# Merged weight products laid after a branch, fetch lists made sooner, first norm on VectorE

## The reference

```
x = x + gelu(layernorm(x) @ ctx.T) @ ctx                     # part 1, per batch
x = x + moe(layernorm(x))                                    # part 2: 8 experts, 256 -> 512 -> 256, one expert per token
x = x + attention(q=layernorm(x), k=v=ctx, 16 heads, mask, distance bias)   # part 3
y = layernorm(x); e = argmax(router(y[:, -1, :]))            # part 4: one expert per batch
x = x + y + 0.3 * ((gelu(y @ W1[e] + b1[e]) @ W2[e] + b2[e]) @ Wo + bo)
```

## Time and profile before

| | |
|---|---|
| median of 3 runs | 701.96 us |
| the profiled execution | 699.54 us, span 697.6 us |
| PE busy | 634.7 us (91%) |
| DVE busy | 325.5 us (47%) |
| ACT busy | 268.8 us (39%) |
| POOL busy | 120.8 us (17%) |
| expert loop, first product to the last pass's end | 284.7 to 370.5 us |
| first query product of attention | 398.88 us |

### The profile page before, as it was taken

The page is one execution under the profiler, slowest core; times in us unless marked ns, Lnnn a source line. Parts: engine busy times, 40 slices in busy tenths (PEclk is TensorE's granted clock), DMA queues, the critical chain, the costliest instruction groups (busy, mean ns, idle before and its releaser), DMA issues.

```text
span 697.6 us, 9158 instructions
## 1 busy us (share of the span) xinstructions
PE 634.7 (91%) x3091; PEld 389.6 (56%) x3093; DVE 325.5 (47%) x1035; ACT 268.8 (39%) x370; POOL 120.8 (17%) x176
## 2 busy tenths in 40 slices
PE   3999999999998779899989668999999989999998
PEld 1666666666666446788878423433433433435665
DVE  4334233103005777122222729768797796752401
ACT  1111111111112233333332256767576577585321
POOL 0000000000002001344452007041022022033310
PEclk9999999999999899999999979999999999999999
DMA  8993301804002314153324395332751600031241
GB/s 306 358 366 117 131 0 68 266 0 155 30 1 75 129 54 145 30 134 122 119 72 144 139 123 84 51 63 44 116 82 25 106 2 3 2 94 43 69 128 60
DMA packets 50086, 70.77 MB, mean 101 GB/s; under 512 B 7472, under 2 KB 39130, under 8 KB 49642
## 3 DMA queue, kind: packets, MB, share of 16 engines
q1 hardware_dynamic: 47898, 64.45, 34.1%
q0 software_dynamic: 2144, 5.77, 3.0%
HBM read 48.48 MB, written 15.13 MB: 91 GB/s over the span
## 4 chain that ended last, share of the span: by engine, by line
PE 70%; DVE 16%; issue 6%; DMA 3%; ACT 2%; POOL 2%; DVEq 0%; POOLq 0%; ACTq 0%; SPq 0%
PE ps L909 14%; PE ps L920 13%; DVE arena L2158 7%; PE ps L1475 6%; PE ps L1089 4%; PE ps L1457 4%; PE ps L1001 4%; PE ps L1200 4%; PE ps L1361 3%; PE ps L1212 3%; PE ps L1097 3%; DVE arena L1874 3%; PE ps L1384 2%; PE ps L1125 1%; PE ps L987 1%
## 5 line engine op out<-in xcount | busy, mean ns | idle before, releaser
L2158 DVE TENSOR_REDUCE arena<-ps 128x1 f32<-128x400 f32 x256 | 129.2, 564 | 41.8 <-PE ps L1361 40.9
L1699 ACT ACTIVATE arena<-ps 100x1024 f32<-100x1024 f32 x128 | 124.0, 1020 | 59.3 <-PE ps L1457 59.1
L909 PE MATMUL ps<-xnT,arena 128*128 128x512 f32 x208 | 102.0, 615 | 0.9 <-DVE xnT L1759 0.9
L920 PE MATMUL ps<-arena 128*128 128x256 f32 x416 | 99.0, 382 | 0.0
L920 PEld LDWEIGHTS ps<-arena 128*128 128x128 f32 x416 | 80.1, 193 | 33.4 <-issue 25.0
L1511 ACT ACTIVATE arena<-ps 128x512 f32<-128x512 f32 x52 | 31.0, 597 | 175.1 <-PE ps L909 175.1
L1361 PE MATMUL ps<-arena 97*128 97x400 bf16 x256 | 76.0, 339 | 6.1 <-DVE arena L2158 2.3
L1457 PE MATMUL ps<-arena 100*100 100x512 bf16 x256 | 75.9, 380 | 0.1
L1475 PE MATMUL ps<-arena 100*32 100x512 f32 x512 | 68.6, 604 | 0.6 <-ACT arena L1699 0.6
L1361 PEld LDWEIGHTS ps<-arena 97*128 97x128 bf16 x256 | 20.4, 97 | 78.2 <-DVE arena L2158 50.1
L909 PEld LDWEIGHTS ps<-xnT,arena 128*128 128x128 f32 x208 | 39.8, 195 | 30.7 <-issue 28.5
(11 more groups left out here) (239 smaller groups left out, 715.9 us busy)
## 6 DMA issues: line engine op xcount, KB each, us to landing
arena<-in_W SPq DMA_DIRECT2D x16, 512.0 KB, 9.2
arena<-in_ctxT SPq DMA_DIRECT2D x4, 1664.0 KB, 8.5
arena<-in_ctxN SPq DMA_DIRECT2D x4, 1664.0 KB, 12.8
arena<-arena SPq DMA_DIRECT2D x48, 128.0 KB
last_k_parts<-arena SPq DMA_DIRECT2D x24, 100.0 KB, 1.8
arena<-last_k_parts SPq DMA_DIRECT2D x8, 300.0 KB
x_tok<-in_x SPq DMA_DIRECT2D x4, 512.0 KB, 9.3
xn_rows<-xn SPq DMA_DIRECT2D x4, 512.0 KB
```

The lines of the kernel that those rows point to most:

```text
L909: ins = pe.matmul(ps[:, 4 + k % 2, :], ctxT_s[:, b % 2, c, f * P:f * P + P], xnT[:, c, S * b:S * b + S], start=(c == 0), stop=(c == KC - 1))
L920: ins = pe.matmul(ps[:, b % 2 * 2 + t // 2, t % 2 * D:t % 2 * D + D], hid[:, (k - 2) % 4, t * P:t * P + P], ctxN_s[:, b % 2, f, :], start= ...
L1699: act.activation(pexp2[0:KT, c % 4, :, :], ps[0:KT, 2 + 2 * (c % 2):4 + 2 * (c % 2), :], ACT.Exp).then_inc(f_pe, 1)
L2158: dve.tensor_reduce(nm2[:, m // MU % 2, h, j:j + 1], ps[:, FAST.bank(x), 0:KF], AX.X, ALU.max, negate=True).then_inc(s_by["dve"], 1)
```

## The change

- Ahead of the loop three merged weights are made instead of four. The fourth, n = 3, follows the loop. n = 4 to 6 stand at the start of the chosen way, behind the branch, in place of the 14 products of `keep_busy`. n = 7 is made after the query products of batch 0 and their splitting. ACT's takes and SP's stores move alike; the store of n = 0 goes ahead of the stores of the keys.
- In the loop DVE makes the list of tokens to fetch after the first W1 copy and not after the second. For that the second copy waits until the first turned block is there.
- POOL runs one pass less in its loop; the last pass has its two scatters alone. SP waits for two fewer loads.
- The norm of batch 0 is applied by DVE and not by ACT, and the two halves of the turned tokens go to banks 6 and 7.
- The bounds given for the value of `pairs` become 8 to 12 from 1 to 12.

```diff
-MERGED_EARLY, MERGED_BIAS = 4, 3
+MERGED_EARLY, MERGED_BIAS, MERGED_LAST = 3, 3, 7
-    early = [(("queries", b, k), 6) for b in range(2) for k in range(KC)]
+    early = [(("queries", b, k), 6 + k) for b in range(2) for k in range(KC)]
...
+            store_merged(0)
             for b in range(B):
                 store_keys(b)
...
-            for n in range(MERGED_EARLY):
-                sp.wait_ge(s_xsb, 32 * (5 + n))
+            for n in range(1, MERGED_EARLY):
+                sp.wait_ge(s_xsb, 32 * (4 + n))
                 store_merged(n)
...
+                store_late_merged()
                 for half in range(2):
                     queries(0, half)
+                store_last_merged()
...
-            sp.wait_ge(s_xsb, pairs * 32 + 64)
+            sp.wait_ge(s_xsb, pairs * 32 + 32)
...
+            def store_late_merged():
+                sp.wait_ge(s_w2s, 16 * (MERGED_EARLY + 1))
+                for n in range(MERGED_EARLY, MERGED_LAST):
+                    store_merged(n)
+
+            def store_last_merged():
+                sp.wait_ge(s_w2s, 16 * (MERGED_LAST + 1))
+                store_merged(MERGED_LAST)
...
             merge_weights(2, 2)
-            pe.wait_ge(s_w2c, merged(1))
-            merge_weights(3, 4)
...
-            merge_weights(4, 2)
+            merge_weights(3, 2)
             pe.wait_ge(s_xsT, pairs * 2 + 2)
             pe.wait_ge(s_expd, 1)
-            merge_weights(5, 4)
-            pe.wait_ge(s_w2c, merged(4))
-            merge_weights(6, 2)
-            pe.wait_ge(s_w2c, merged(5))
-            merge_weights(7, 4)
+
+            def merge_late():
+                merge_weights(4, 4)
+                pe.wait_ge(s_w2c, merged(3))
+                merge_weights(5, 2)
+                pe.wait_ge(s_w2c, merged(4))
+                merge_weights(6, 4)
+
+            def merge_last():
+                pe.wait_ge(s_w2c, merged(6))
+                merge_weights(MERGED_LAST, 4)
...
-                pe.wait_ge(s_gat[0], 16)
-                keep_busy(2)
-                pe.wait_ge(s_moe, 1)
-                keep_busy(8)
-                pe.wait_ge(s_lnst, 2 * 0 + 1)
-                keep_busy(4)
+                merge_late()
                 pe.wait_ge(s_tpf, tp[0])
                 for k in range(KC):
                     make(("queries", 0, k))
                 queries(0)
                 query_rest(0)
                 query_rest(1)
+                merge_last()
                 for k in range(KC):
                     make(("queries", 1, k))
...
-                act.wait_ge(s_w2s, 16 * (E + 1) if b else 16 * (MERGED_EARLY + 1))
+                act.wait_ge(s_w2s, 16 * (MERGED_EARLY + 1, MERGED_LAST + 1, MERGED_LAST + 1, E + 1)[b])
...
             def fast_way():
-                norm(0, 0, 1)
+                take_late_merged()
                 for k in range(KC):
                     take_columns(("queries", 0, k))
                 query_parts()
+                take_merged(MERGED_LAST, 4)
                 norm(1, 0, B)
...
+            def normalize(b):
                 for t in range(TB * b, TB * b + TB):
                     ins = dve.tensor_scalar(xn[:, t, :], x_tok[:, t, :], mv[:, t, 0:1], rstd[:, t:t + 1], ALU.subtract, ALU.mult)
                 ins.then_inc(s_ln, 1)
...
             with dve.Fori(0, pairs) as i:
-                for j in range(2):
-                    dve.wait_ge(s_eh, i * 2 + j + 1)
-                    block_weights(bass.ds(i * 2 + (2 + j), 1), j)
+                dve.wait_ge(s_eh, i * 2 + 1)
+                block_weights(bass.ds(i * 2 + 2, 1), 0)
                 dve.wait_ge(s_xsTr, i * 2 + 3)
                 dve.tensor_scalar(idx_x[:, :], idx[:, bass.ds(i * 2 + 4, 2)], 0.0, None, ALU.add).then_inc(s_idxl, 1)
+                dve.wait_ge(s_eh, i * 2 + 2)
+                block_weights(bass.ds(i * 2 + 3, 1), 1)
...
                 norm_roots(0)
+                if first_norm:
+                    dve.wait_ge(s_w2s, 16 * (MERGED_EARLY + 1))
+                    normalize(0)
                 norm_shifts(0)
...
-            with pool.Fori(0, pairs) as i:
+            with pool.Fori(0, before_last) as i:
...
+            pool.wait_ge(s_idx, before_last + 1)
+            pool.sem_inc(s_turn, 1)
+            for j in range(2):
+                pool.wait_ge(s_eyc, before_last * 2 + j + 1)
+                pool.sem_inc(s_turn, 1)
+                store_answers(j)
```

More of the change, by code:

```diff
@@ L29 @@
 NBLK = 24
-PAIRS = NBLK // 2
+PAIRS, LEAST_PAIRS = NBLK // 2, T // P // 2
 IDX = NBLK + 4
@@ L681, in _ @@
             sp.wait_ge(s_slot, 1)
-            pairs = sp.value_load(be_i[0:1, NBLK:NBLK + 1], min_val=1, max_val=PAIRS)
+            pairs = sp.value_load(be_i[0:1, NBLK:NBLK + 1], min_val=LEAST_PAIRS, max_val=PAIRS)
             sp.wait_ge(s_list, 1)
@@ L828, in _ @@
                 sp.dma_start(yg[:, TB * b:TB * b + TB, :], yt_d[S * b:S * b + S, :].rearrange("(t p) d -> p t d", p=P)).then_inc(s_gat[b], 16)
-            sp.wait_ge(s_w2s, 16 * (MERGED_EARLY + 1))
-            for n in range(MERGED_EARLY, E):
-                store_merged(n)
+            def store_late_merged():
[5 more added lines that the diff above has]
+                store_merged(MERGED_LAST)
             with sp.If(near > 0):
@@ L1075, in _ @@
             pe.wait_ge(s_slot, 1)
-            pairs = pe.value_load(be_i[0:1, NBLK:NBLK + 1], min_val=1, max_val=PAIRS)
+            pairs = pe.value_load(be_i[0:1, NBLK:NBLK + 1], min_val=LEAST_PAIRS, max_val=PAIRS)
             pe.wait_ge(s_w12, 16 * 2 * E)
@@ L1117, in query_products @@
                 if b == 0:
-                    pe.wait_ge(s_w2c, merged(E - 1))
+                    pe.wait_ge(s_w2c, merged(5))
+                if b == 1:
+                    pe.wait_ge(s_w2c, merged(MERGED_LAST))
                 for m in range(KC):
@@ L1553, in _ @@
             act.activation(bo2[:, :], ps[0:E, 0, 0:D], ACT.Copy, scale=0.3).then_inc(s_w2c, 1)
-            for n, bank in ((2, 2), (3, 4)):
-                take_merged(n, bank)
+            take_merged(2, 2)
             act.wait_ge(s_slot, 1)
@@ L1558, in _ @@
                 act.wait_ge(s_ekst[i], 48 * KC * B // 2)
-            pairs = act.value_load(be_i[0:1, NBLK:NBLK + 1], min_val=1, max_val=PAIRS)
+            pairs = act.value_load(be_i[0:1, NBLK:NBLK + 1], min_val=LEAST_PAIRS, max_val=PAIRS)
             with act.Fori(0, pairs) as i:
@@ L1569, in _, with take_late_merged @@
             act.sem_inc(s_expd, 1)
-            for n, bank in ((4, 2), (5, 4), (6, 2), (7, 4)):
-                take_merged(n, bank)
+            def take_late_merged():
+                for n, bank in ((3, 2), (4, 4), (5, 2), (6, 4)):
+                    take_merged(n, bank)
             act.wait_ge(s_list, 1)
@@ L1754, in layer_norm @@
                 ins.then_inc(s_ln, 1)
+            def layer_norm(b):
+                norm_roots(b)
+                normalize(b)
             def take_columns(b, bank=6):
@@ L1939, in _ @@
             ch.step(dve, dve.tensor_reduce(need[:, 0:1], pw[:, :], AX.X, ALU.add))
+            dve.tensor_scalar(be_i[:, NBLK + 1:NBLK + 2], need[:, 0:1], -1.0, None, ALU.add)
             dve.tensor_copy(be_i[:, NBLK:NBLK + 1], need[:, 0:1]).then_inc(s_slot, 1)
@@ L1955, in _ @@
                 dve.tensor_copy(xsT[:, j, :, :].rearrange("p k n -> p (k n)"), ps[:, 6 + j, 0:KC * P]).then_inc(s_xsT, 1)
[L1956 removed]
+            pairs = dve.value_load(be_i[0:1, NBLK:NBLK + 1], min_val=LEAST_PAIRS, max_val=PAIRS)
             with dve.Fori(0, pairs) as i:
[L1958 to L1960 removed]
+                dve.wait_ge(s_eh, i * 2 + 1)
+                block_weights(bass.ds(i * 2 + 2, 1), 0)
                 dve.wait_ge(s_xsTr, i * 2 + 3)
                 dve.tensor_scalar(idx_x[:, :], idx[:, bass.ds(i * 2 + 4, 2)], 0.0, None, ALU.add).then_inc(s_idxl, 1)
+                dve.wait_ge(s_eh, i * 2 + 2)
+                block_weights(bass.ds(i * 2 + 3, 1), 1)
                 for j in range(2):
@@ L2048, in general_way @@
             def general_way():
-                add_all_experts()
+                add_all_experts(False)
                 for b in range(B):
@@ L2148, in fast_way @@
                 cf = Chain(f_dv)
-                add_all_experts()
+                add_all_experts(True)
                 dve.memset(nmb2[:, :, :, :], 0.0)
@@ L2286, in _ @@
             pool.wait_ge(s_slot, 1)
-            pairs = pool.value_load(be_i[0:1, NBLK:NBLK + 1], min_val=1, max_val=PAIRS)
+            before_last = pool.value_load(be_i[0:1, NBLK + 1:NBLK + 2], min_val=LEAST_PAIRS - 1, max_val=PAIRS - 1)
             pool.wait_ge(s_xsTr, 2)
```

6 lines of the change are left out of this document (2 added, 4 removed).

## The result

The changed kernel takes 679.38 us (median of 4 runs, 679.05 to 680.86), the kernel before beside it 701.67 (699.81 to 702.20): ratio 0.972, interval 0.9693 to 0.9747 (the medians alone give 679.38 / 701.67 = 0.968, just outside it; a repeat on another chip, below, gave 0.975 with 680.8 us). Faster, as forecast, but by 22.3 us and not by 8.1. The time is 14.5 us under the forecast and 10.6 under the lower end of its range (690 to 698). The profiled execution took 679.57 us with a span of 677.7, against 699.54 and 697.6 before.

A forecast was written before the change was run, and what follows sets the result against it. From 266 to 430 us PE was taken to carry the end nearly everywhere, partly without useful work. Terms -2.56 + 0.3 - 7.8 + 2.0 = -8.1 took 701.96 to 693.9 us, range 690 to 698.

The forecast's parts named there:

- Start of the loop: Ahead of the loop: without n = 3, blocks turn at 278.95 instead of 281.51, 3.19 us entry kept; gain 2.56 us.
- The loop: Nine loop passes: earlier gathers remove waits, but the second gelu's 5.19 us takes that back; +0.3 us in all.
- Rival (1): In the loop: passes gain too, all nine at 8.08 us, -3.9 instead of +0.3, 689.7 us; chance 0.13.
- Loop's end to S: Loop's end to first query product (S): four merges 13.81, branch 2.7, slow products 1.5, ACT's part; 20.5 us, gain 7.8.
- The cover: Behind the loop: DVE's answers, roots and norm end at 15.6 us, hidden by PE's merges ending at 18.0; 2.4 spare.
- S to the second product: First query product (S) to second: n = 7 now stands out by 2.0 us, 15.7 us instead of 13.66.
- Rivals (2) to (5): After loop: branch dear on PE, 697.5 (0.13); branch free, 690.9 (0.05). Loop slower, 704.4 (0.05). Nothing moves, 702 (0.04).
- Rival (4): In the loop: second W1 copy and a gather wait on the path, 1.2 us longer per pass, 704.4 us; chance 0.05.

The follow-up runs named there:

- e1b: Kernel before with only the fetch list moved after the first W1 copy, where the kernel before takes 698.36 us: 690.63 us, ratio 0.9888.
- e2b: Changed kernel with the fetch list back after the second W1 copy, where the kernel before takes 698.36 us: 687.0 us, ratio 0.9827.
- e12: Changed kernel with two POOL memsets ahead of each pass's gathers, so its gathers and scatters come about 1.2 us later: 686.31 us, ratio 0.978.
- e5: Changed kernel with merged weight n = 3 made ahead of the loop again: 685.52 us, ratio to before 0.9802.
- e6: Changed kernel with merged weight n = 7 made right behind n = 6, ahead of batch 0's queries: 684.12 us, ratio to before 0.9796.
- e11: Kernel before with POOL's last scatter of each pass held until the next pass's second gelu: 695.04 us, ratio 0.9925.
- e1: Kernel before with only the fetch list moved after the first W1 copy, where the kernel before takes 693.03 us: 690.37 us, ratio 0.9966.
- e2: Changed kernel with the fetch list back after the second W1 copy, where the kernel before takes 693.03 us: 679.73 us, ratio 0.9797.
- e4: Changed kernel with two POOL memsets ahead of each pass's first scatter: 680.09 us, ratio 0.981; repeated where the kernel before takes 700.94 us: 680.0 us.
- e9: Changed kernel with idle products before the first turned blocks, batch 1's roots made earlier and its norm ahead of n = 7's take: 675.51 us, ratio 0.9674.
- e9b: Second run of the changed kernel with idle products, batch 1's roots made earlier and its norm ahead of n = 7's take: 675.97 us, ratio 0.9626.
- b0: Kernel before, unchanged, run again with its own profile on another chip: 699.6 us, ratio 1.0004.
- e10: Kernel before with the stores of the four early merged weights all moved behind the loop: 699.05 us, ratio 1.0007.

## Why the prediction was right or wrong

- **Start of the loop: right.** Forecast 282.14, measured 282.32. One half was off against the other: TensorE still waited 2.20 us for the gathered rows and turned the blocks at 280.39, not at 278.95, but the entry after it took 1.93 and not 3.19. The first rows' landing had been read too early from the earlier trace rows: its digits show nothing under a tenth, while in the same view's GB/s row 23 GB/s still flow until 279.15, and in the changed kernel the chain has the rows there only at 280.26.
- **The loop: wrong, and with it the forecast.** The step that failed is "what the gather gives back the late gelu takes: passes of both kinds last the same". Forecast +0.3 us, measured -8.9. I took the gelu at 5.19 us for a property of the pass, against which an earlier list could do nothing. It was the late signal, and the list's place made it. By that edit the loop takes 77.9 us (e1b) against 82.2 to 85.7, and 82.9 (e2b) against 76.8 to 77.5; e12 brings the late signals back with the burst's old time. The earlier trace rows held the hint. The products took 3.81 us, and the gelu that needs only them began at 5.19; a release 1.4 us after the work is done is not the work's price. Rival (1), the loop gains, had the sign but only -3.9, by the best pass of before (8.08), and that pass was disturbed too. Without a late signal it is 7.46. The gather waits that I did count are small beside this: TensorE's weight loads for the turnings waited 2.6 us in all for gathered rows in the loop of before. No run here says what holds the signal, so that part of the cause is open.
- **Loop's end to S: right in mechanism, 1.6 too little.** Merges n = 3 to 6 are in the chain above with two gaps, 0.85 + 1.48 = 2.33 against 2.7. Of the 1.5 us for slow products behind the gap 0.5 came: the four merges took 3.45 + 1.99 + 8.91 = 14.35 us in place of 13.81, and the eight products behind the gap 0.25 each, not the 0.39 of the idle products before. ScalarE's part behind the merges was 2.19 in place of 2.52. The Trainium skill (Runtime: NRT & Kernel Launch, Instruction fetch mechanics) has a taken branch stop an engine until a DMA has brought the page. The trace agrees with the gap of 0.85 at the branch, and its queues move instructions there (361 to 363 us) and again from 364 to 367; whether the second gap, eight products behind the branch, is such a stop it doesn't say.
- **The cover: right, but thinner.** VectorE's norm took 1.38 us, under the 1.67 assumed, and ended 375.44, TensorE's merges 375.95. That is 0.5 us of cover where 2.4 were forecast. Of the 1.9 us, 1.3 are TensorE's: its merges ended 16.7 us after the loop's end and not 18.0. The other 0.6 are VectorE's (16.2 and not 15.6): its answers arrived 9.05 us after the loop's end, only 0.3 sooner than before and not 1.2. e5 takes the cover away and VectorE is late by 3.4 us.
- **S to the second product: right up to the turnings, 1.2 too dear.** 14.47 against 15.7. The norm of batch 1 ended at S + 12.5 (forecast 12.7). The term that was mis-sized is the two turnings, put at 2 x 1.12: they took 1.09 together, 390.73 to 391.82, at the full granted clock and without a second wait, and the copies followed at 391.42. The 0.8 us against the kernel before is not the price of n = 7, which by e6 is 2.1 to 2.5; the rest is won back by the turnings.
- **Rivals (2) to (5): none came.** The branch cost neither 6.3 nor nothing. Rival (4) needed the second W1 copy on the path; it starts 5.05 us into the pass at 341.73, where the late pass of e2b above has it at 5.87, and TensorE doesn't wait for it. (Its limit is 8.4 / 9 = 0.93 a pass, not 0.94.)

## What to carry to other kernels

In a loop whose DMA issues depend on its own signals, compare the time from a producer's end to its consumer's start with the same step elsewhere in the pass. Where it is longer, it is a delay that can go, and not a term of the sum. Then move a part of the burst away: here gathers 1.2 us earlier (e12 against the changed kernel) or a last scatter 2.2 us later (e11) each brought the signal back nearly in time. Read a pass that is free of the delay, not the best of the disturbed ones. Where an experiment shows nothing, look first whether the unchanged kernel on that chip has the delay at all (e1, e2). And before a stretch is shortened, work out which engine comes last once it is: here VectorE ended only 0.5 us ahead of TensorE, and the same merge taken from the stretch gained nothing (e5).

## What the runs showed of the hardware

- TensorE's signal to ScalarE and VectorE came up to 1.9 us late (5.65 against 3.77 us into a pass) where POOL's two gathers and two scatters were issued back to back over it. This was so on the chips on which the kernel before takes 698 to 702 us. On one chip it takes 693.03 (689.98 to 695.65, 19 runs), and none of the four traces from there (e1 to e4) has a late signal. Yet e2's burst there (-1.12 to 2.74) is one that went with 4.65 to 4.77 in single passes elsewhere. The changed kernel hardly tells the chips apart: 679.38 and 680.8, and 680.09 and 680.0 with the memsets of e4.
- TensorE waited for 2.20 us and, after four turnings, for 1.30 more. The stretch of the first pass then shows a granted clock of 0.78 of full speed (2.4 GHz), so a part of it ran at the lower level of 1.2 GHz, and the pass took 9.17 us. With idle products in place of the first wait it shows 1.00 and took 7.54 (e9 and e9b). The wait does not settle the level by itself. In before and b0, the same kernel with the same 2.59 us of wait ahead of its first product, the stretch from 284.6 to 292.2 us shows 0.78 in one and 1.00 in the other, and the first pass took 9.17 and 7.54. Of the ten traces with the waits of the changed kernel none was under 8.88, so that the idle products brought the 7.54 is likely, on two traces.
- POOL's record of the last scatter took 0.99 us in undisturbed passes of the changed kernel and up to 1.42 in the late ones of before. This doesn't go with the late signal: e4's took 1.13 to 1.38 in seven passes with gelu 2 at 3.77, and e12's about 0.99 in eight late ones. It goes with VectorE's W1 copy. Over the loops of all 20 traces 148 of POOL's gathers and scatters took over 1.05 us, and each has such a copy lying over part of it; of the 515 without one none did. The Trainium skill (Perfetto Trace Analysis, DMA Instruction — SWDGE (GPSIMD)) says that such a record ends when the descriptors are written, not when the data has moved. The trace agrees. A late pass of e10 has in its timeline

```profile
346.36 1.29 POOL L2279 DMA_INDIRECT answers_by_token<-arena,tokens_to_store  x1 [0.30 <-issue]
...
348.25 0.60 ACT L1563 ACTIVATE arena<-ps 128x512 f32<-128x512 f32 x1 [2.38 <-PE ps L1089]
```

and in the DMA view of 343.2 to 351.5 us (busy tenths in 40 slices of 0.21 us)

```profile
DMA  0000245455377300791000009800000000000000
```

The record ends at 347.65, and the last busy slices, the 25th and 26th, begin at 343.2 + 24 x 0.2075 = 348.18. The gelu is released at nearly the same moment, 348.25. But nothing else ties the two: in pass six of the same trace the gelu starts at 331.65, and the last scatter's data moves only from 332.25 (the 36th of 40 slices of 327 to 333 us). So the start of this movement isn't what releases it.
